# The tail of a mixture-of-experts routing stage: another order on four engines, logits and row numbers selected straight from PSUM, region offsets in the running sums

## The reference, cut to what matters

```python
logits = xs @ Wg                                  # 608 x 8
probs = softmax(logits)
topv, topi = top_k(probs, 2)
cw = topv / sum(topv)                             # weights of the two experts
eid_flat = topi.T.reshape(-1)
dispatch_mask = argsort(eid_flat)                 # rows sorted by expert
dispatched = xs[dispatch_mask % S]
for e in range(8):                                # each expert on its own rows
    h = relu(dispatched @ W1[e] + b1[e])
    expert_outputs += sel_e * (h @ W2[e] + b2[e])
# weighted by cw, added back to its token
```

## Time and profile before

| | |
|---|---|
| median of 3 runs | 257.41 us (256.68, 257.41, 260.4) |
| the profiled execution's own time | 256.9 us, of which the span is 255.1 us |
| busy share of the span | PE 86%, DVE 55%, ACT 43%, POOL 29% |
| share of the chain that ended last | PE 73%, DVE 8%, DMA 7%, ACT 4% |
| mean granted TensorE clock | 0.872 of full speed |

### The profile page before, as it was taken

One profiled execution on the slowest core, in us unless ns is written; L12 is line 12 of the kernel. 1 busy time (PEld: TensorE's weight loads), 2 busy tenths in 40 slices (PEclk: granted clock), 3 DMA queues, 4 the chain that ended last, 5 costly groups with the idle time before them and its releaser, 6 DMA issues.

```text
span 255.1 us, 4433 instructions
## 1 busy us (share of the span) xinstructions
PE 219.5 (86%) x1340; PEld 189.2 (74%) x1340; DVE 141.2 (55%) x422; ACT 110.8 (43%) x252; POOL 74.7 (29%) x109
## 2 busy tenths in 40 slices
PE   7397797995999999999999773599999999999940
PEld 6286496663887967878879561489999999999930
DVE  5345248696567858657456459765776433424200
ACT  2334366864143443735326595245433424334210
POOL 4003350372004060413322363002332423324240
PEclk9659599996799999999795555579999999999996
DMA  7999999999500000000100596532342342431313
GB/s 131 188 234 159 262 291 270 265 215 255 195 10 0 0 4 1 0 3 0 31 4 26 172 318 163 134 95 49 52 59 39 57 54 37 67 44 18 31 15 89
DMA packets 26259, 25.73 MB, mean 101 GB/s; under 512 B 4971, under 2 KB 23262, under 8 KB 26222
## 3 DMA queue, kind: packets, MB, share of 16 engines
q1 hardware_dynamic: 22333, 22.17, 35.6%
q0 software_dynamic: 3568, 2.64, 8.2%
q10 hardware_dynamic: 336, 0.66, 1.5%
HBM read 16.57 MB, written 7.77 MB: 95 GB/s over the span
## 4 chain that ended last, share of the span: by engine, by line
PE 73%; DVE 8%; DMA 7%; ACT 4%; issue 3%; SPq 2%; POOL 1%; DVEq 0%; ACTq 0%; POOLq 0%
PE ps L973 12%; PE ps L950 12%; PE ps L708 7%; PE ps L712 6%; PE ps L798 5%; PE ps L580 4%; PE ps L784 4%; PE ps L962 4%; PE ps L677 4%; DMA ximg<-in_x 3%; PE ps L691 2%; PE ps L681 2%; DMA sent<-row,index 1%; PE ps L572 1%; DMA sums<-ys,xs 1%
## 5 line engine op out<-in xcount | busy, mean ns | idle before, releaser
L1640 POOL DMA_INDIRECT sums<-ys,xs x17 | 26.3, 1546 | 66.6 <-ACT ys L1537 57.1
L973 PE MATMUL ps<-w2s,hidT 128*128 x204 | 36.1, 327 | 1.1 <-DVE hidT L1341 0.8
L973 PEld LDWEIGHTS ps<-w2s,hidT 128*128 128x128 f32 x204 | 33.0, 189 | 2.1 <-issue 1.6
L950 PE MATMUL ps<-w1hi,xhi 128*128 x68 | 25.3, 372 | 1.0 <-ACT xend L1530 0.7
L1537 ACT ACTIVATE ys<-ps,xs 128x192 f32<-128x192 f32 x17 | 7.2, 421 | 39.9 <-PE ps L973 37.6
L1320 DVE TENSOR_TENSOR xlo<-ps,xhi 128x128 fp32r<-128x128 f32 x17 | 5.0, 292 | 28.2 <-ACT xend L1530 28.2
L1627 POOL COPY vexp<-vtok 114x32 f32<-114x32 f32 (+1 forms) x36 | 8.0, 222 | 42.6 <-PE ps L712 40.6
L1419 ACT ACTIVATE qlb<-ps,cst 96x228 f32<-96x228 f32 (+1 forms) x36 | 12.1, 426 | 16.8 <-PE ps L746 16.8
L1147 DVE TENSOR_TENSOR kvb<-ps,cst 96x288 f32<-96x288 f32 (+1 forms) x24 | 10.0, 418 | 16.1 <-PE ps L784 16.1
L708 PE MATMUL ps<-at,vexp 114*96 114x114 f32 (+1 forms) x144 | 18.7, 286 | 0.0
L784 PE MATMUL ps<-vm,ktok 114*96 114x288 f32 (+1 forms) x48 | 15.6, 406 | 2.7 <-DVE kvb L1147 2.7
(11 more groups left out here) (192 smaller groups left out, 473.1 us busy)
## 6 DMA issues: line engine op xcount, KB each, us to landing
w2s<-in_L_ffn_W SPq DMA_DIRECT2D x8, 576.0 KB
sent<-blank SPq DMA_DIRECT2D x1, 3977.0 KB, 32.5
w1s<-in_L_ffn_W SPq DMA_DIRECT2D x4, 768.0 KB, 16.6
xs<-sent SPq DMA_DIRECT2D x17, 96.0 KB, 2.0
w1s<-in_L_ffn_W SPq DMA_DIRECT2D x4, 384.0 KB, 18.1
w1hi<-w1hi SPq DMA_DIRECT2D x8, 192.0 KB
ximg<-in_x SPq DMA_DIRECT2D x12, 96.0 KB, 7.9
w1s<-in_L_ffn_b SPq DMA_DIRECT2D x1, 792.0 KB
```

Source lines behind the costliest of these rows:

```text
L950: last = pe.matmul(ps[2 + c][:, 0:PASS], xx, of_expert(ww, expert), start=(n == 0), stop=(n == len(products) - 1))
L973: last = pe.matmul(ps[6 + j % 2][:, 0:D], hidT[:, k, :], of_expert(w2s[:, :, k, :], expert), start=(k == 0), stop=(k == FCH - 1))
L1640: po.indirect_dma_start(sums, bass.IndirectOffsetOnAxis(ap=xs[:, j % NS, D + TAIL + 1:].bitcast(U32), axis=0), ys[:, j % 2, :], None, comp ...
```

## The change

It does six things. (1) `take_logits` and `take_places` go: the search for the largest and its numbers reads the logits in `ps[1]`, and the selection of row numbers reads `ps[4]`. (2) The region offset moves from a constant that DVE added to each group's places into row 0 of the first running sum (POOL writes it once), and the constant `full` that the counts are compared with carries it too. (3) The difference of the two largest goes: ACT's exponential takes the second as its bias and scales the first by -1. (4) `send` is split in `shares` (the weights), `send` (row numbers) and `combine` (the combine row), and the semaphore `dv_row` that releases a scatter is raised by the row numbers. (5) The places of all parts in the steps change: DVE's `route` of a group stands at the end of the step of its logits, its `shares`, `send` and `combine` in m = 2 of the next step, between `windows` of m = 2 and `own_blocks` of m = 3; PE's `places` in m = 1 of the next step; ACT's `weight` ahead of `heads_out`. (6) In the last two steps the order is written out anew: on PE the biases of the first four groups come behind the last `places`, and on POOL scatter 3 comes ahead of the last `copy_row`.

Core of the diff:

```diff
-                pe.wait_ge(dv_both, 2 * g + 2)
+                pe.wait_ge(dv_both, 2 * g + 1)
                 pe.wait_ge(dv_key_sums, GROUPS)
...
+                    if m == 1 and 0 <= t - 6 < GROUPS - 3:
+                        places(t - 6)
...
-                if t - 5 == GROUPS - 1:
-                    places(GROUPS - 2)
-                    output_biases(range(4))
-                if 0 <= t - 6 < GROUPS - 3:
-                    places(t - 6)
                 if 0 <= t - 4 < GROUPS:
                     project_out(t - 4)
                 if t == GROUPS + 3:
+                    places(GROUPS - 2)
                     turn_combine(range(4))
                 if 1 <= t < GROUPS - 3:
...
             places(GROUPS - 1)
+            pe.wait_ge(dv_both, 2 * GROUPS)
             pe.matmul(ps[0][0:1, 0:E], ones[:, 0:1], run[:, GROUPS, :], start=True, stop=True).then_inc(pe_counts, 1)
+            output_biases(range(4))
             turn_combine(range(4, GROUPS))
             output_biases(range(4, GROUPS))
...
+            def route(g):
 
                 n = group(g)[1]
+                found = ps[1][0:n, 256:256 + E]
                 ve.wait_ge(pe_logits, g + 1)
-                ve.tensor_copy(logit[0:n, g, :], ps[1][0:n, 256:256 + E]).then_inc(dv_logits, 1)
-
-            def take_places(g):
-
-                n = group(g)[1]
-                ve.wait_ge(pe_places, g + 1)
-                ve.tensor_tensor(slot[0:n, g, :], ps[4][0:n, 0:E], const("region")[0:n, :], ALU.add).then_inc(dv_places, 1)
...
+                ve.max(top[0:n, g, :], found).then_inc(dv_top, 1)
+                ve.wait_ge(dv_top, g + 1)
+                ve.max_index(topi[0:n, g, :], top[0:n, g, :], found).then_inc(dv_logits, 1)
                 ve.wait_ge(dv_logits, g + 1)
-                link(ve.max(top[0:n, g, :], logit[0:n, g, :]))
-                link(ve.max_index(topi[0:n, g, :], top[0:n, g, :], logit[0:n, g, :]))
...
-                ve.tensor_tensor(diff[0:n, g, 0:1], top[0:n, g, 1:2], top[0:n, g, 0:1], ALU.subtract).then_inc(dv_diff, 1)
...
+            def shares(g):
+
+                n = group(g)[1]
+                ve.wait_ge(ac_weight_exp, g + 1)
+                link(ve.tensor_scalar(share[0:n, g, 1:2], share[0:n, g, 0:1], 1.0, None, ALU.add))
+                link(ve.reciprocal(row[0:n, g, 0, D:D + 1], share[0:n, g, 1:2]))
+                ve.wait_ge(gp_row, g + 1)
+                link(ve.tensor_tensor(row[0:n, g, 1, D:D + 1], row[0:n, g, 0, D:D + 1], share[0:n, g, 0:1], ALU.mult))
+
             def send(g):
 
                 n = group(g)[1]
+                ve.wait_ge(pe_places, g + 1)
+                ve.tensor_tensor(pick[0:n], sel[0:n, g], ps[4][0:n, 0:E].unsqueeze(1).broadcast_to([n, TOP, E]),
+                                 ALU.mult).then_inc(dv_places, 1)
                 ve.wait_ge(dv_places, g + 1)
-                link(ve.tensor_tensor(pick[0:n], sel[0:n, g], slot[0:n, g, :].unsqueeze(1).broadcast_to([n, TOP, E]), ALU.mult))
                 with nc.allow_low_precision(reason="row numbers: whole, one term of each sum is not zero"):
-                    link(ve.tensor_reduce(index[0:n, g, :], pick[0:n], AX.X, ALU.add))
-                ve.wait_ge(ac_weight_exp, g + 1)
-                link(ve.tensor_scalar(diff[0:n, g, 2:3], diff[0:n, g, 1:2], 1.0, None, ALU.add))
-                link(ve.reciprocal(row[0:n, g, 0, D:D + 1], diff[0:n, g, 2:3]))
-                ve.wait_ge(gp_row, g + 1)
-                ve.tensor_tensor(row[0:n, g, 1, D:D + 1], row[0:n, g, 0, D:D + 1], diff[0:n, g, 1:2], ALU.mult).then_inc(dv_row, 1)
-                ve.wait_ge(dv_row, g + 1)
-                link(ve.tensor_scalar(pick[0:n, 0, :], sel[0:n, g, 0, :], row[0:n, g, 0, D:D + 1], None, ALU.mult))
-                ve.scalar_tensor_tensor(comb[0:n, g, :], sel[0:n, g, 1, :], row[0:n, g, 1, D:D + 1], pick[0:n, 0, :],
+                    ve.tensor_reduce(index[0:n, g, :], pick[0:n], AX.X, ALU.add).then_inc(dv_row, 1)
+
+            def combine(g):
+
+                n = group(g)[1]
+                link(ve.tensor_scalar(part[0:n], sel[0:n, g, 0, :], row[0:n, g, 0, D:D + 1], None, ALU.mult))
+                ve.scalar_tensor_tensor(comb[0:n, g, :], sel[0:n, g, 1, :], row[0:n, g, 1, D:D + 1], part[0:n],
                                         ALU.mult, ALU.add).then_inc(dv_combine, 1)
                 ve.wait_ge(dv_combine, g + 1)
...
-                        route(t - 6)
-                    if m == 1 and 0 <= t - 7 < GROUPS - 4:
-                        send(t - 7)
+                    if m == 2 and 0 <= t - 6 < GROUPS - 3:
+                        shares(t - 6)
+                        send(t - 6)
+                        combine(t - 6)
                 if t == GROUPS + 3:
-                    take_places(GROUPS - 3)
+                    shares(GROUPS - 3)
                     send(GROUPS - 3)
-                    take_logits(GROUPS - 2)
+                    combine(GROUPS - 3)
+                    route(GROUPS - 2)
+                    shares(GROUPS - 2)
                 if 0 <= t - 4 < GROUPS:
                     residual(t - 4)
+                if t == GROUPS + 2:
+                    route(GROUPS - 3)
+                    tokens_out(GROUPS - 2)
                 if t == GROUPS + 3:
+                    send(GROUPS - 2)
                     tokens_out(GROUPS - 1)
-                    route(GROUPS - 2)
-                if 0 <= t - 5 < GROUPS - 2:
-                    take_logits(t - 5)
-                if 0 <= t - 6 < GROUPS - 3:
-                    take_places(t - 6)
-                if t == GROUPS + 2:
-                    tokens_out(GROUPS - 2)
-                    route(GROUPS - 3)
-                    send(GROUPS - 4)
+                    combine(GROUPS - 2)
                 if t < GROUPS:
                     features(t)
...
                 t0, n, _ = group(g)
-                ac.wait_ge(dv_diff, g + 1)
-                ac.activation(diff[0:n, g, 1:2], diff[0:n, g, 0:1], ACT.Exp).then_inc(ac_weight_exp, 1)
+                ac.wait_ge(dv_top, g + 1)
+                ac.activation(share[0:n, g, 0:1], top[0:n, g, 0:1], ACT.Exp, bias=top[0:n, g, 1:2],
+                              scale=-1.0).then_inc(ac_weight_exp, 1)
...
                 if t == 3:
                     xhat_out(5)
+                if 0 <= t - 6 < GROUPS - 2:
+                    weight(t - 6)
                 if t == GROUPS + 3:
-                    weight(GROUPS - 3)
...
                     ac.wait_ge(w1_in, 16 * E)
                     weights_high(0)
+                    weight(GROUPS - 2)
                     root(GROUPS - 1, 1)
+                    combine_out(0)
                     x2_out(GROUPS - 1)
-                    weight(GROUPS - 2)
-                    combine_out(0)
+                    weight(GROUPS - 1)
...
             po.wait_ge(sent_blank, 16)
-            for g in range(GROUPS - 4, GROUPS + 2):
-                if g < GROUPS:
-                    copy_row(g)
-                scatter(g - 2)
+            copy_row(2)
+            scatter(0)
+            copy_row(3)
+            scatter(1)
+            copy_row(4)
+            scatter(2)
+            scatter(3)
+            copy_row(5)
+            scatter(4)
+            scatter(5)
             po.wait_ge(sums_in, 16 * (GROUPS + 1))
```

More of the change, by code:

```diff
@@ L182, in build @@
         comb = sb("comb", [GTOK, GROUPS, E])
-        logit = sb("logit", [GTOK, GROUPS, E])
-        slot = sb("slot", [GTOK, GROUPS, E])
+        part = sb("part", [GTOK, E])
         top = sb("top", [GTOK, GROUPS, E])
@@ L1270, in _ @@
                     embedded(3)
[L1271 removed]
+                if 0 <= t - 5 < GROUPS - 3:
+                    route(t - 5)
             route(GROUPS - 1)
[L1273 to L1275 removed]
+            shares(GROUPS - 1)
             send(GROUPS - 1)
+            combine(GROUPS - 1)
             attention_over(ve)
```

25 lines of the change are left out of this document (8 added, 17 removed).

## The result

The change makes the kernel slower: 262.09 us median (261.14 to 264.41, 4 runs) against 258.9 us (256.68 to 263.39, 4 runs) beside it, a ratio of 1.0196 with a 95% interval of 1.0153 to 1.024. Run again later it was 262.67 us, ratio 1.0244 (1.0161 to 1.0327). Every ratio here leaves out executions in a slower state (for the kernel before, 263.39 is one), so it is not the quotient of the two medians. The profiled execution took 261.81 us, of which the span is 260.0; that of before had 256.9 and 255.1. I had forecast 256.3, in a range of 253.9 to 259.2.

The account below looks back on a forecast made before the run. PE was taken to bound the kernel, except for DVE's residual ending steps 6 and 7 and the last scatter's landing. 256.9 + 1.1 (middle) - 1.9 (end) = 256.1 profiled; forecast measured time 256.3 us, range 253.9 to 259.2.

Parts of the forecast that it names:

- The end's steps: End of the routing: last scatter starts 3.24 us earlier, first tile load at 156.87 instead of 158.77, gaining 1.9 us.
- I take the row's 3.70: End of the routing: the last scatter still lands 3.70 us after its issue, as in the profile before.
- a rival, at 0.05: End of the routing: scatters land late or loads wait for something else; the end gains 0, 258.0 us; chance 0.05.
- bounded it by 1 us: End of the routing: the gain falls to 0.9 us if the landing takes 1 us more among the weights' traffic.
- The first term of the middle: Step 6: ACT's later exponential and DVE's seven instructions in m = 2 make residual 0.70 us late.
- My bound of 1.8 for the whole middle: Middle: costs up to 1.8 us if later residuals also hold up the moments, ACT's roots and copies.
- The second term: Step 7: the exponential is again last before DVE's seven instructions, making residual 0.43 us late.
- slower, by one mechanism: End of step 6 or 7: PE's longer wait brings one more lower-clock stretch, costing 1.7 us, 257.8; chance 0.18.
- The stretch of before behind step 7: Lower clock in most of 124 to 128 us, such a stretch priced at 1.7 us; it may fall away or move.
- The table load: ACT in the middle: each load ahead of the exponential costs 1.29 us, without the skill page's added drain.
- that drain: ACT's table switches: the skill page adds about 1380 ns of drain each, making the middle cost about 3.9 us.
- The range: Whole kernel: 253.9 to 259.2 us, the top being the slower case with middle at 1.8 and half the runs' spread.

Follow-up runs that it names:

- POOL's wait: The changed kernel, with GpSimd's masked values (vm) of the last group waiting for DVE's first combine; median 260.11 us (4 runs), no ratio given.
- the middle mended: The changed kernel, with ACT's weight at the start of the step and POOL's vm waiting until the first comb is written; 257.81 us, ratio 0.9991.

## Why the prediction was wrong, point by point

Two steps failed. At the end it is the landing. In the middle it is two terms that the sum does not have: POOL beside DVE's small instructions, and the clock behind PE's longer wait.

- **The end's steps were right up to the landing.** The last issue was to come 3.24 earlier with the tokens 0.56 later, 3.80 against the tokens; it came 3.83 earlier. Step 9 is 0.51 longer (I had about 0.56 for `shares` ahead of `residual`). ACT's rounding and SP's copies end as forecast.
- **The step that failed at the end** is "I take the row's 3.70". I took a landing from a moment at which the DMA share was 0.75 and applied it 3.8 us earlier against the tokens, where it is above 1.0. It was 7.63, and the end gained nothing instead of 1.9. I did name this as a rival, at 0.05, and in the term itself had bounded it by 1 us. The windows of before show the traffic: a share of 1.03 or more in each us from 145 to 152. The scatter was moved into the tail of that, and it was what the first tile load waited for last. That w2 is the traffic that matters is shown: with two or all four of the late loads moved away the landing came back to 3.8 and 4.0.
- **The first term of the middle** (0.70 in step 6) was right for what it was made of, but left out a resource: 0.65 was found for it, and 1.34 more because POOL's vm held two DVE instructions. My bound of 1.8 for the whole middle had another reason (held-up moments and roots). The row of vm stood in the trace of before, at 107.40 to 109.76, and seven DVE instructions were being moved beside it.
- **The second term** (0.43 in step 7) was right: 0.40.
- **The clock** was the rival "slower, by one mechanism", at 0.18 and 1.7 us. It is what both profiles of the change show, dearer than I priced it: 16.11 less 13.38 is 2.7 us for one stretch from 110.8 to 117.8, since it lasted 7 us where the stretch of before that I had priced lasted 3.5. PE waited 2.19 us ahead of it, where before had 0.54 and I expected some 1.2. The stretch of before behind step 7 did not come, which gives 1.23 back in step 8; I had allowed for both and summed neither. That 1.23 is no gain of the change: in the five profiles with its end and the middle put back, step 8 took 11.15 to 13.23, and in two with its middle 18.00 and 19.27.
- **The table load** costs its 1.28 and no drain: the exponential starts 0.01 to 0.02 behind it in every profile. With that drain I had reckoned 3.9 for the middle, and 3.9 is what steps 6 to 8 cost; that is chance, since no term of it is a drain.
- **The sum as it should have been**: 256.9 + 0.65 + 1.34 (POOL) + 0.40 + 2.73 (clock) - 1.23 (the old stretch) + 0.51 + 0.09 + 0.4 (ahead of step 6 and in the tiles, together) = 261.8, the profiled execution. The parts are read from this same profile and two others, so the sum is an account and no test.
- **The range.** Its upper end does not follow from its words: 257.8, 0.7 for the middle at its bound and half of the runs' spread, 1.86, make 260.4, not 259.2. The measured 262.09 lies above either.

My range had room for one bad case at a time. A late `residual` and a fall of the clock have PE's wait in common, so they were not two independent mishaps, and the end's gain was priced without a look at what else moved then.

## What to carry to other kernels

When small instructions move, look at what every other engine does at the new place, not only at the dependencies: a GpSimd instruction that reads SBUF can turn a 0.16 us instruction of VectorE into one of 0.8. A transfer's time belongs to the moment it was measured in; when its issue moves, read the DMA share of the new moment first. And price a longer wait of TensorE twice, once for itself and once for the clock behind it, from several profiles: one profile can show the fall in another place than the next.

## What the runs showed of the hardware

- Two small DVE instructions, L1194 and L1209, took 0.81 and 0.91 us beside POOL's vm and 0.16 and 0.22 without it, while `pick` and `index` between them took 0.17 each.
- Behind PE's wait for `residual` of step 6 the granted clock stood at 1.2 GHz from 110.8 to 117.8 in the change (wait 2.19 us, and the same in its repetition), from 111.5 to 118.5 with POOL's wait (0.86 us), and from 111.5 to 115.0 in the kernel before with w2 later (0.54 us). It stayed at 2.4 GHz in the change with w2 later (2.19 us), with eight products filled in (0.41 us), in the kernel before and with the middle mended (0.54 us both). It is not a matter of the wait's length alone. The same four matmuls L769 took 1.01 us at the lower level and 0.58 at the upper.
- The same indirect DMA, 38 rows, took between 3.42 and 8.18 us from issue to landing, by what else the DMA engines moved: 5.86 with all of w2 ahead of it, 3.81 with 1.2 MB of it less. In eight profiles with all of w2 ahead it spread from 5.86 to 8.18 for a cause that stays open.
